# State steps 20 to 31 turned as two accumulated products, and the orders of all queues written anew (one core, Trainium2)

## What is computed

```
y  = x @ W[subject].T + b[subject]                  # a 256x256 matrix for each sequence, 8 subjects
q, k, v = y @ Wq.T+bq, y @ Wk.T+bk, y @ Wv.T+bv      # 16 heads of 16
sim = q k^T / 4 / (|temperature| + 0.1)
scores = sum over 5 freqs of a[h,f] * sin(2*pi*sim/freq + p[h,f])
w = sigmoid(scores); w = w / (sum(w) + 1e-10)
x = x + layernorm(w v @ Wo.T + bo) * gamma + beta
# the second half
h = relu(x @ W1[lang] + b1[lang]); r = x + h @ W2[lang] + b2[lang]
z = layernorm(r) * gamma[lang] + beta[lang]
for n in range(32):                                  # the batch axis is the time of a recurrence
    f, i = sigmoid(z[n] @ wf.T + c @ uf.T + bf), sigmoid(z[n] @ wi.T + c @ ui.T + bi)
    g = tanh(z[n] @ wc.T + c @ uc.T + bc)
    c = f * c + i * g                                # c is 64 x 256
x = x + tanh(z @ wo.T + c_final @ uo.T + bo)
```

## Time and profile before

| | |
|---|---|
| three runs | 341.22, 341.5, 343.73 us; median 341.5 |
| profiled execution | 340.6 us, of which the span of the trace is 338.8 us |
| busy in the span | PE 277.5, DVE 286.6, ACT 270.2, POOL 56.0 us |
| mean granted TensorE clock | 0.948 of full speed |

### The profile page before, as it was taken

How to read it: one execution, slowest core, us unless ns; L and a number is a source line. 1 busy time by engine, 2 the same in 40 slices (tenths; PEclk the granted TensorE clock), 3 DMA queues, 4 the chain that set the end, 5 groups by cost and what they waited for, 6 DMA issues and landing times.

```text
span 338.8 us, 7109 instructions
## 1 busy us (share of the span) xinstructions
PE 277.5 (82%) x2532; PEld 164.0 (48%) x2532; DVE 286.6 (85%) x617; ACT 270.2 (80%) x405; POOL 56.0 (17%) x58
## 2 busy tenths in 40 slices
PE   5846768466869889998988988989898998999890
PEld 5735337343437754545455544545663454433350
DVE  2179995998987999999999998999999999454356
ACT  1299698989998999999999999999999974323123
POOL 5000000222020002234400316033013321210000
PEclk9999796758797999999999999999999999999997
DMA  5688046592033455416514320651144161010006
GB/s 168 205 268 321 1 67 178 111 263 55 0 57 102 71 157 159 70 41 119 110 21 99 103 33 1 142 102 17 18 127 86 32 134 25 3 31 0 2 17 231
DMA packets 32229, 31.74 MB, mean 94 GB/s; under 512 B 10690, under 2 KB 24130, under 8 KB 32194
## 3 DMA queue, kind: packets, MB, share of 16 engines
q1 hardware_dynamic: 27266, 26.46, 29.3%
q0 software_dynamic: 4352, 4.20, 8.1%
q10 hardware_dynamic: 576, 0.64, 0.7%
HBM read 23.15 MB, written 2.10 MB: 75 GB/s over the span
## 4 chain that ended last, share of the span: by engine, by line
ACT 42%; DVE 27%; PE 14%; issue 11%; DMA 3%; POOL 2%; SPq 1%; DVEq 0%; ACTq 0%; POOLq 0%
ACT ang L1102 13%; ACT ang L1111 11%; DVE sc L1619 8%; PE pg L674 4%; ACT sc L1093 3%; DVE ang L1604 2%; ACT gat L1157 2%; DVE fc L1761 2%; PE pf L584 2%; ACT sc L1122 2%; PE pf L504 2%; DVE ang L1595 2%; PE pr L626 2%; ACT L1108 2%; ACT L1115 2%
## 5 line engine op out<-in xcount | busy, mean ns | idle before, releaser
L1619 DVE SCALAR_TENSOR_TENSOR sc<-ang,small,sc 128x512 f32<-128x512 f32 (+1 forms) x160 | 98.3, 637 | 1.3
L1111 ACT ACTIVATE ang<-ang,qs 128x2560 f32<-128x2560 int32 x32 | 77.0, 2427 | 1.5 <-DVE ang L1604 1.4
L1102 ACT ACTIVATE ang<-sc,phase 128x512 int32<-128x512 f32 (+1 forms) x126 | 72.3, 644 | 0.0
L674 PE MATMUL pg<-gate_u,cT 128*64 128x384 f32 x256 | 48.0, 496 | 5.0 <-DVE cT L1770 5.0
L665 PE MATMUL pg<-gate_w,zT 128*64 128x384 f32 x256 | 50.1, 498 | 0.8 <-DVE zT L1751 0.7
L1604 DVE TENSOR_SCALAR ang<-ang 128x2560 int32<-128x2560 int32 x32 | 47.2, 1484 | 0.9 <-ACT ang L1102 0.8
L1157 ACT ACTIVATE gat<-pg 128x384 f32<-128x384 f32 x32 | 15.5, 485 | 26.8 <-PE pg L674 26.8
L1595 DVE TENSOR_SCALAR ang<-sc,phase 128x256 int32<-128x256 f32 (+1 forms) x74 | 28.1, 417 | 5.2 <-ACT sc L1093 5.1
L584 PE MATMUL pf<-qm,kT 64*64 64x128 f32 x512 | 19.8, 298 | 11.3 <-DMA qm<-qT 3.3
L674 PEld LDWEIGHTS pg<-gate_u,cT 128*64 128x64 f32 x256 | 16.1, 136 | 26.2 <-issue 16.0
L665 PEld LDWEIGHTS pg<-gate_w,zT 128*64 128x64 f32 x256 | 15.5, 136 | 19.6 <-issue 14.7
(11 more groups left out here) (111 smaller groups left out, 464.4 us busy)
## 6 DMA issues: line engine op xcount, KB each, us to landing
wc<-in_cond SPq DMA_DIRECT2D x30, 257.0 KB, 3.6
w<-in_up SPq DMA_DIRECT2D x32, 128.2 KB, 2.7
wa<-in_down SPq DMA_DIRECT2D x32, 66.0 KB, 2.2
xt<-in_xt SPq DMA_DIRECT2D x8, 256.0 KB, 3.9
xt<-rows POOLq DMA_DIRECT2D x8, 256.0 KB, 4.9
w<-x POOLq DMA_DIRECT2D x8, 256.0 KB, 4.0
xg<-in_x SPq DMA_DIRECT2D x3, 512.0 KB, 4.8
qm<-qT SPq DMA_DIRECT2D x48, 32.0 KB, 2.1
```

What stands on the lines that cost most here:

```text
L674: mm = pe.matmul(pg[n % 2][u * L:(u + 1) * L, 0:GCOLS], cT[:, kc, :], gate_u[:, kc, u, :], start=False, stop=(kc == KC - 1), skip_group_ch ...
L1102: op = act.activation(ang[:, n % SLOTS, f, r], unit(n)[:, r], ACT.Identity, scale=TURN / FREQS[f], bias=phase[:, p * NF + f:p * NF + f + 1])
L1111: act.activation(a.bitcast(F32), a, ACT.Sin, scale=2 * PI_LOW / TURN, bias=qs[:, 3:4]).then_inc(sine_ready, 1)
L1619: op = dve.scalar_tensor_tensor(out=unit(n)[:, r], in0=sine, scalar=amp, in1=unit(n)[:, r], op0=ALU.mult, op1=ALU.add)
```

## The change

Two things in one edit. `LATE` goes from 32 to 20: steps 20 to 31 turn the state as the sum of two products, and PE then waits for `cell_step(n, 0)` and not for `cell_step(n, 1)`. And the call lists of all five engines are written in a new order, with the same calls in them, except that on ACT `sines(31, False)` and `weights(30, False)` become `True`: two more table loads. The helpers `shifted_wait` and `added_wait` and an unused tuple come in without changing a wait that runs.

```diff
-LATE = 32
+LATE = 20
+ADDED_BY_DMA = ()
@@ (sync)
-            load_x(1)
-            load_cond(1, 2)
             load_cond(1, 3)
             load_cond(1, 0)
             load_cond(1, 1)
+            load_x(1)
+            load_cond(1, 2)
@@ (tensor, the last steps; the same for steps 29, 30 and 31)
             output_projection(7, 0)
             output_projection(7, 1)
-            input_gates(23, 1)
             state_gates(23)
...
             input_gates(28, 0)
+            state_turned(27)
             input_gates(28, 1)
-            state_turned(27)
             state_gates(28)
@@ (scalar)
             gates(19)
-            sines(31, False)
+            angle(31, 4)
             weights(28, True)
             weights(29, False)
             gates(20)
+            sines(31, True)
             residual_turned(6)
+            gates(21)
+            weights(30, True)
+            weights(31, False)
             keep_output_part(5)
-            gates(21)
-            weights(30, False)
-            weights(31, False)
@@ (vector, the start)
             conditioned(0)
             mask_queries(0)
+            mask_queries(1)
             angle(0, 0)
             angle(0, 1)
             angle(0, 2)
-            mask_queries(1)
-            wrap(0)
             angle(1, 0)
             angle(1, 1)
             angle(1, 2)
+            wrap(0)
@@ (vector, part 3)
             add_sine(22, 0)
             cell_step(10, 0)
             add_sine(22, 1)
+            normalise(3)
...
-            moments(3, 1)
-            add_sine(22, 2)
-            wrap(24)
-            normalise(3)
```

More of the change, by code:

```diff
@@ L289, in slot_free, with shifted_wait, added_wait @@
                 eng.wait_ge(score_ready, added(m))
+        def shifted_wait(eng, q):
+            if q in SHIFT_BY_DMA:
+                eng.wait_ge(xt_shifted[q % 2], 16 * count(SHIFT_BY_DMA, q))
+            else:
+                eng.wait_ge(xt_ready, sum(k not in SHIFT_BY_DMA for k in range(q + 1)))
+        def added_wait(eng, q):
+            if q in ADDED_BY_DMA:
+                eng.wait_ge(x1_moved[q % 2], 16 * count(ADDED_BY_DMA, q))
+            else:
+                eng.wait_ge(x1_ready, sum(k not in ADDED_BY_DMA for k in range(q + 1)))
         def kept(q):
@@ L817, in _ @@
             state_turned(1)
-            scores(9)
-            input_gates(2, 0)
             input_gates(2, 1)
             state_gates(2)
+            scores(9)
+            turn_residual(1)
+            input_gates(3, 0)
+            input_gates(3, 1)
+            adapter_down(1)
             condition(5, 0)
@@ L1275, in _ @@
             angle(10, 4)
+            residual_turned(0)
+            sines(8, False)
             angle(11, 1)
@@ L1433, in _ @@
             angle(27, 4)
-            queries(4, 0)
+            sines(26, False)
+            gates(14)
             keys(4, 0)
-            gates(14)
-            sines(26, False)
             sines(27, False)
@@ L1683, in residual_added @@
                 dve.wait_ge(x1_part, q + 1)
-                if q in SHIFT_BY_DMA:
-                    dve.wait_ge(xt_shifted[q % 2], 16 * count(SHIFT_BY_DMA, q))
-                else:
-                    dve.wait_ge(xt_ready, sum(k not in SHIFT_BY_DMA for k in range(q + 1)))
+                shifted_wait(dve, q)
                 dve.tensor_tensor(x1[:, part(q)], x1[:, part(q)], xt[:, q % 2], ALU.add).then_inc(x1_ready, 1)
@@ L1945, in _ @@
             add_sine(14, 0)
-            angle(16, 0)
+            angle(15, 0)
             add_sine(14, 1)
             add_sine(14, 2)
+            angle(16, 0)
+            add_sine(14, 3)
+            angle(16, 1)
+            cell_step(2, 0)
+            hidden(1, 0)
             add_sine(13, 4)
-            cell_step(2, 0)
+            add_sine(14, 4)
+            hidden(1, 1)
+            wrap(15)
             cell_step(2, 1)
-            add_sine(14, 3)
-            wrap(15)
-            hidden(1, 0)
@@ L1955, in _ @@
-            angle(16, 1)
+            wrap(16)
+            adapted(1)
+            moments(1, 0)
             state_copy(2)
             angle(17, 0)
-            hidden(1, 1)
-            wrap(16)
-            add_sine(14, 4)
-            adapted(1)
+            moments(1, 1)
             conditioned(3)
-            moments(1, 0)
             add_sine(15, 0)
-            moments(1, 1)
             add_sine(15, 1)
+            normalise(1)
+            add_sine(15, 2)
+            add_sine(15, 3)
@@ L1967, in _ @@
+            add_sine(16, 0)
+            add_sine(16, 1)
+            cell_step(3, 0)
+            cell_step(3, 1)
+            residual(2)
+            residual_added(2)
+            add_sine(15, 4)
             angle(18, 0)
             angle(18, 1)
-            add_sine(15, 2)
-            normalise(1)
-            add_sine(15, 3)
-            add_sine(16, 0)
-            cell_step(3, 0)
+            modulated(1)
+            shifted_language(1)
             divided(6, 0)
+            add_sine(16, 2)
@@ L2062, in _ @@
             angle(24, 0)
+            wrap(23)
+            hidden(3, 0)
+            angle(24, 1)
+            hidden(3, 1)
             state_copy(9)
-            wrap(23)
-            angle(24, 1)
-            add_sine(21, 4)
-            hidden(3, 0)
-            hidden(3, 1)
+            wrap(24)
+            adapted(3)
+            moments(3, 0)
+            moments(3, 1)
             add_sine(22, 0)
@@ L2256, in _ @@
             shifted_language(7)
+            cell_step(26, 1)
             cell_step(27, 0)
```

767 lines of the change are left out of this document (379 added, 388 removed).

## The result

The changed kernel takes 347.36 us at the median of four runs (345.69 to 348.64), the kernel before 342.52 us beside it (341.22 to 343.73): ratio 1.0127, 95% interval 1.0086 to 1.0167. By the ratio it is slower by about 4.3 us (the two medians are 4.8 apart); the forecast of 341.4 us and its range (337 to 345.5) both miss. The profiled execution took 348.55 us, its span is 346.7 us.

The account below looks back on a forecast made before the run. DVE and ACT were taken as bound, then two chains and the recurrence. Form 0.0, last steps +0.5, attention's end +0.15, start -0.5, POOL -0.2 on 340.6 gave 340.55, on the median's scale 341.4 us; range 337 to 345.5.

Parts of the forecast that it names:

- The step to start from: DVE until its last sine sum: its list is a sum of durations, so `add_sine(31, 4)` moves only by idle time.
- The sign that the prediction named for it: Changed trace: a shift of `weights(31)` by over 2 us would show the forecast wrong, through the order in the full stretch.
- The start: `mask_queries(1)` ahead of the first angles: +1.2 us at 50 us, then recovered; -0.5 us, bounds +1.2 and -3.
- The step's form: Turning the state by two products: 0.32 us saved by earlier release, 0.33 more on PE; net 0.0 a step.
- The last steps: Steps 28 to 31: half of the input gates stands between turned state and state gates; +0.5 us, bounds 0 and +0.8.
- The end of the attention: Last sigmoids to `gates(27)`: recurrence gains up to 0.9 us, part 7's chain is delayed; +0.15, bounds -1.0 and +1.5.
- POOL and the wrap: POOL's small add beside DVE's wrap: part 3 gains 0.9 us, part 0 loses some 0.9 at most; -0.2 taken.
- Rival 1: DVE waits at `cell_step(n, 0)` for late tanhs, so `weights(31)` comes 3.5 to 5 us later: 345.5 us; chance 0.16.
- Rival 3: The start's delay is not recovered: 341.4 + 1.7 = 343.1 us, still no change; chance 0.09.
- Rival 4: Products cost the skill page's price, 0.44 us more on ten serial steps from `weights(31)` on: 345.8 us; chance 0.03.
- The scale: Profiled execution of 340.6 us taken as 0.9 below the median of 341.5, to put the forecast on the median's scale.

Follow-up runs that it names:

- e3: Changed kernel with the heads of all five lists (127 calls of DVE, to about 114 us) from before; 346.96 us, ratio 1.0104.
- e1: Changed kernel with LATE back at 32: new orders, transposes, `cell_step(n, 1)` directly behind `cell_step(n, 0)` from step 20; 347.37 us, ratio 1.0106.
- e7: Kernel before with 23 DVE calls moved by one place, so that 26 more dependent pairs stand directly behind one another; 345.92 us, ratio 1.0066.
- e6: Changed kernel with 37 exchanges of neighbours on DVE that take adjacent dependent pairs apart; 346.31 us, ratio 1.0072.
- e9: e3 with 26 exchanges of neighbours on DVE (from the 117th call to the last sine sum 64 pairs become 34); 346.0 us, ratio 1.0104.
- e10: e3 with ACT's list from its 265th call on as before, without the two added table loads; 353.4 us, ratio 1.0345.
- e12: Kernel before with 15 exchanges on DVE, `wrap(24)` behind `normalise(3)` and the ends of PE and DVE new; 349.71 us, ratio 1.0241.
- e2: Kernel before, in its old orders, with LATE at 20 alone (products instead of transposes); 345.65 us, ratio 1.0037.

## Why the prediction was wrong

- **The step to start from.** "DVE's list is a sum of durations": the durations of instructions were right, but I took their sum as independent of order. The sum of the ends and starts between neighbours is not: 17 more adjacent dependent pairs are worth 1.9 us, and durations and waits hardly differ. The step "All calls ahead of `add_sine(31, 4)` on DVE are the same set as before, so its place in time moves only by idle time" is the one that failed, for 2.29 us; e3 (2.03) shows it without the changed head and e1 (2.75, of which some 0.2 is the one call more) without the form. The sign that the prediction named for it, `weights(31)` over 2 us late, is there: 7.18 us in the profiled execution, about 3 of them the head's luck. e7 shows the price of the pairs. That they alone hold the new order back is not shown: e6 and e9 took out more pairs than the 17 that the changed order has on top, and DVE then waited for the other engines and the DMAs instead. So the new order loses on their side as well, and why it does there stays open.
- **The start**, -0.5 with bounds -3 and +1.2: +1.1 to +1.6, with an error of 0.6 to 0.9, so at the unfavourable bound or outside it; the sign was wrong. The walk was right to the first sine (1.45 forecast, 1.41 measured against the first conditions), and right that ACT gains later by filling its waits: at `squares(0)` it stood 1.6 behind the trace of before after 3.5. Then the walk has nothing of what came next, 3.1 us lost by the place of `angle(11, 4)`: PE waits for conditions, its clock at 0.50, late tokens and queries. I walked durations from a trace in which PE ran the queries at full clock, though that is the smaller part (up to 0.5 us in the old order).
- **The step's form**, 0.0 with bounds -0.05 and +0.2: 0.23 in the old order. Two sizes were off. The product pair takes 0.39 more than the transpose up to the copy, not 0.33. In the changed kernel the four records of a pair start at 320.51, 320.72, 320.83 and 320.94: 0.11 apart as in the warm-up rows, but 0.21 behind the first one. And in the old order PE is not free 0.49 after `fc`. In the new one it is, and the 0.48 there is the forecast.
- **The last steps**, +0.5 with bounds 0 and +0.8: +0.88. The mechanism was right, a half of the input gates between the turned state and the state gates; the half could start 0.64 behind the product's first record (321.15), not 0.44: 0.10 more behind the first record and 0.10 more behind the last.
- **The end of the attention**, +0.15: -0.19 from the last sine sum to `gates(27)`. Right in kind: both table loads are hidden, `gates(23)` gains 0.64 on `weights(31)` and `gates(25)` 1.36, and part 7's chain then takes most of it back.
- **POOL and the wrap**, -0.2: about 0. `normalise(3)` no longer waits (0.88 before), `normalise(0)` waits 0.92 (before 0.07) for a root whose add ran beside the wrap, as forecast. By the rows of part 0 POOL's add ends at 99.69 (98.33 and 1.36) and the wrap at 99.61 (98.15 and 1.46). The rule that the forecast cited from the Trainium skill, "SBUF — State Buffer", section "SBUF: two separate sides", would have part 0 lose what part 3 gains; the trace agrees, 0.92 against 0.88. In both parts POOL's add ended just behind the wrap (0.08 and 0.04 us), though in the earlier trace rows it had started 0.46 ahead of it; starts on POOL are rough.
- **The rivals.** Rivals 1 (345.5) and 4 (345.8) were near in size, but neither was the mechanism; that the sizes met is chance. Rival 1: DVE doesn't stand behind the recurrence in the changed kernel. It does in e10 and e12. Rival 3 (the start's delay stays) fits the +1.1 to +1.6 of the start, but not the rest. Rival 4 is refuted: the pair and the hop to DVE take 0.75 together, less than the 0.88 of rival 4 for the pair alone. So the four times of the Trainium skill, "TensorE: Matmul & The Clock Gate", Terms, is not what these traces show, which have about twice: two records a product and one a transpose, and 0.75 against 0.36 to the copy for two products against one transpose.
- **The scale.** I put the profiled execution 0.9 us below the median of three runs. It was the earliest of eleven at the 101st call, 1.9 below their mean, and the medians of before beside the later experiments were 343.5 to 344.2. Ratios are not touched by this, but the forecast in microseconds was 1 us low against the 342.52 of its own comparison and about 2 us against the later ones.

## What to carry to other kernels

A list of the same instructions on a full engine does not have the same length in another order: count the neighbours that wait for one another directly (here 0.11 us each) before you call an engine's time a sum. Where two or three engines are full side by side, taking time out of one list returns as its waits, and an order can be slower on more than one of them; undoing one part, even an apparently wasteful one such as a table load, can cost far more than it frees. And before walking from one trace, take several of the same kernel and see how far the stretch that you walk from varies.

## What the runs showed of the hardware

- **The head's spread goes with the first load and the clock.** The eleven traces of the old head end the same 101 calls up to 3.9 us apart. `conditioned(0)` is done between 12.76 and 14.89 us; counted from there the spread is 2.5. In some traces PE runs the first values at half clock; how much of the rest that makes is not shown. Before, then e2 and e10, the window from 22 to 30 us (the clock is the number ahead of the last two):

```profile
22.00:30.00 8.00, 4.52 (x78) 3.88 (x80) 7.64 (x20) 8.00 (x16) 0.00 (x0) 1.00 0.95 327
```

```profile
22.00:30.00 8.00, 4.66 (x66) 3.98 (x64) 6.27 (x15) 7.89 (x16) 0.00 (x0) 0.79 0.90 277
```

```profile
22.00:30.00 8.00, 4.79 (x64) 4.20 (x64) 6.09 (x14) 8.00 (x16) 0.00 (x0) 0.63 0.93 302
```

  The 32 matmuls of `values(0)` took 1.97 us in before and 3.30 in e2, with the same order ahead of them. Why the granted clock falls at a different moment from one execution to the next isn't shown.
- **Two neighbours on DVE overlap by 0.08 us** unless the second waits for the first, then they are 0.03 apart (medians over the 317 neighbours from the 117th call to the last sine sum).
- **POOL's small add** took 0.35 us in part 3 without a wrap beside it and 1.36 in part 0 with one (1.98 in the earlier trace rows).
